# Block 3's o times proj as seven products, with proj's weight sums made by GpSimd in blocks 1 to 3

## What is computed

```python
x = L0_attn_x
xn = _layernorm(x, axis=-1)
# inside s: q, k, v = rmsnorm(xn) @ ternary(qkv_w).T; chunk by chunk
#   o = scale * (intra + cross);  S = lam_T * S + kv
#   o = rmsnorm(rmsnorm(o)) @ ternary(proj_w).T
s = _L0_attn_ref(xn, L0_attn_qkv_w, L0_attn_qkv_norm_w, L0_attn_proj_w, L0_attn_proj_norm_w, L0_attn_norm_w, L0_attn_s)
g = _silu(_L0_ffn_ref(xn, L0_ffn_weight, L0_ffn_bias))
x = x + s * g
```

## Time and profile before

| | before |
|---|---|
| median of 3 runs | 1307.04 us (1304.21 to 1307.58) |
| the profiled execution, its own time | 1304.94 us |
| span of the profiled execution, first to last instruction | 1303.7 us |
| busy: PE, DVE, ACT, POOL | 1271.8, 998.4, 741.1, 518.2 us |
| mean granted TensorE clock | 0.997 |

### The profile page before, as it was taken

One profiled execution on the slowest core, in us unless ns is written; L12 is line 12 of the kernel. 1 busy time (PEld: TensorE's weight loads), 2 busy tenths in 40 slices (PEclk: granted clock), 3 DMA queues, 4 the chain that ended last, 5 costly groups with the idle time before them and its releaser, 6 DMA issues.

```text
span 1303.7 us, 26389 instructions
## 1 busy us (share of the span) xinstructions
PE 1271.8 (98%) x10263; PEld 806.5 (62%) x10263; DVE 998.4 (77%) x1552; ACT 741.1 (57%) x1792; POOL 518.2 (40%) x435
## 2 busy tenths in 40 slices
PE   4999999999999999999999999999999999999998
PEld 2576867666665746657565665757566574656655
DVE  7888368677777878789777787878878787878745
ACT  5886256273554646566464566657456464646732
POOL 1430793835434334253432235242243324325161
PEclk9999999999999999999999999999999999999999
DMA  9622211303113031130402103040120404112020
GB/s 360 254 98 74 58 50 34 114 10 106 49 34 113 18 106 34 39 116 18 138 18 89 42 22 133 17 136 20 73 66 17 130 17 127 29 48 75 2 81 33
DMA packets 35677, 97.69 MB, mean 75 GB/s; under 512 B 10977, under 2 KB 11233, under 8 KB 35554
## 3 DMA queue, kind: packets, MB, share of 16 engines
q1 hardware_dynamic: 33024, 88.65, 19.8%
q10 hardware_dynamic: 2530, 7.37, 2.7%
HBM read 71.85 MB, written 16.81 MB: 68 GB/s over the span
## 4 chain that ended last, share of the span: by engine, by line
PE 85%; POOL 4%; DVE 4%; issue 3%; ACT 2%; DMA 1%; SPq 0%; DVEq 0%; POOLq 0%; ACTq 0%
PE ring L866 18%; PE ring L825 13%; PE ring L799 13%; PE ring L851 12%; PE ring L1030 10%; PE att_ps L904 4%; PE ring L1006 3%; PE att_ps L959 3%; PE ring L916 2%; PE att_ps L932 2%; PE att_ps L962 1%; DVE b_lo L1438 1%; PE ring L769 1%; DMA raw<-in_ffn_w 1%; POOL ffn_sum L2452 1%
## 5 line engine op out<-in xcount | busy, mean ns | idle before, releaser
L866 PE MATMUL ring<-b_hi,qkv_q 128*128 128x256 f16 x1216 | 268.2, 272 | 0.8 <-DVE b_lo L1438 0.8
L866 PE MATMUL ring<-b_lo,qkv_q 128*128 128x256 f16 x1216 | 268.2, 273 | 0.0
L2557 POOL TENSOR_TENSOR xt<-xt,gate_even 128x512 f32<-128x512 f32 x58 | 90.1, 1557 | 205.8 <-DVE gate_even L1626 158.0
L2535 POOL TENSOR_TENSOR sq<-sq 128x512 f32<-128x512 f32 (+1 forms) x58 | 58.0, 1000 | 239.8 <-DVE b_lo L1438 143.7
L866 PEld LDWEIGHTS ring<-b_hi,qkv_q 128*128 128x128 fp8e4 x1216 | 120.2, 99 | 17.9 <-DVE b_lo L1438 1.7
L866 PEld LDWEIGHTS ring<-b_lo,qkv_q 128*128 128x128 fp8e4 x1216 | 118.9, 98 | 14.9
L2161 ACT ACTIVATE sq<-att_ps,sq_scale 128x128 f32<-128x128 f32 x256 | 69.9, 381 | 54.3 <-DVE ow L1581 29.7
L2056 ACT ACTIVATE arena<-arena,lam_T 64x64 f32<-64x64 f32 x384 | 93.0, 329 | 4.3 <-issue 3.7
L2546 POOL TENSOR_TENSOR small<-small 128x1 f32<-128x1 f32 x32 | 19.6, 614 | 162.2 <-DVE small L1633 162.2
L2523 POOL TENSOR_TENSOR stack_odd<-arena,lam_q 64x1024 f32<-64x1024 f32 x32 | 82.6, 2581 | 2.9 <-POOL xt L2557 0.3
L2077 ACT ACTIVATE gate_odd<-ring,wscale 128x512 f32<-128x512 f32 x26 | 17.9, 687 | 112.0 <-PE ring L851 112.0
(11 more groups left out here) (305 smaller groups left out, 3561.8 us busy)
## 6 DMA issues: line engine op xcount, KB each, us to landing
xt<-in_x SPq DMA_DIRECT2D x60, 512.0 KB, 4.0
out<-xt SPq DMA_DIRECT2D x31, 512.0 KB, 2.6
raw<-in_qkv_w SPq DMA_DIRECT2D x24, 512.0 KB, 15.8
arena<-arena ACTq DMA_DIRECT2D x28, 256.0 KB, 2.9
y<-in_x_turned SPq DMA_DIRECT2D x14, 512.0 KB, 5.8
y_odd<-in_x_turned SPq DMA_DIRECT2D x14, 512.0 KB, 6.7
raw<-in_ffn_w SPq DMA_DIRECT2D x8, 512.0 KB, 10.0
norm_rows<-norm_out SPq DMA_DIRECT2D x14, 256.0 KB, 5.9
```

The source lines that it names most:

```text
L866: ins = pe.matmul(ring[:, b, e * BT:(e + 1) * BT], qkv_q[:, cb, o:o + P], part[:, cb, :], start=(cb == 0 and part is b_hi and (e == 0 or i ...
L2535: pool.tensor_tensor(sq[:, 0, 0:m, :], sq[:, 0, 0:m, :], sq[:, 0, m:2 * m, :], ALU.add).then_inc(s_sqw, 1)
L2557: pool.tensor_tensor(o, o, gate_of(i)[:, c, cs], ALU.add).then_inc(s_add, 1)
```

## The change

`BY_PRODUCTS` goes from 4 to 3, so block 3's o is multiplied by proj as seven products as well. The four sums of proj's weights move on GpSimd: T1 from block 3, before `decay_q(3, 0)`, to the end of block 1's list, behind `sum_squares(1, 1)`; T2 from behind `decay_q(3, 1)` to block 2, behind the norm factors; T4 from block 4 to block 2's `attention(2, 0)`, behind the sum T3 of k; T3 from block 4 to block 3's `attention(3, 0)`. Two waits in `decay_q` that stood for the old places take the ordinary form.

```diff
@@ -374,7 +374,7 @@
-        BY_PRODUCTS = 4
+        BY_PRODUCTS = 3
@@ -2511,11 +2511,11 @@
                 elif c == 1 and is_first(g - 1):
-                    pool.wait_ge(*((s_zeros, 2) if i == 0 else (s_pwsum, 3)))
+                    pool.wait_ge(s_zeros, CHUNKS)
...
                 elif c == 0:
-                    pool.wait_ge(*((s_pwsum, 1) if i == BY_PRODUCTS - 1 else (s_add, of_out(i - 1, 1, 1))))
+                    pool.wait_ge(s_add, of_out(i - 1, 1, 1))
@@ -2570,7 +2570,7 @@
                     if i == BY_PRODUCTS - 1:
-                        sum_proj_weights("T2")
+                        sum_proj_weights("T4")
                     if i == BY_PRODUCTS:
                         sum_proj_weights("T3")
@@ -2587,6 +2587,8 @@
                     sum_squares(i, 1)
+                    if i == 1:
+                        sum_proj_weights("T1")
@@ -2643,6 +2645,8 @@
                         norm_scale(i + 1, 0)
                         norm_scale(i + 1, 1)
+                    if i == 2:
+                        sum_proj_weights("T2")
@@ -2659,10 +2663,6 @@
                         add_out(i - 1, 1, 1)
-                        if i == BY_PRODUCTS - 1:
-                            sum_proj_weights("T1")
-                        if i == BY_PRODUCTS:
-                            sum_proj_weights("T4")
                         decay_q(i, 0)
                         decay_q(i, 1)
```

## The result

| | kernel before | changed kernel |
|---|---|---|
| median of 22 runs each, us | 1307.96 (1303.17 to 1309.62) | 1308.99 (1308.42 to 1311.28) |
| profiled execution, us (its span) | 1304.94 (1303.7) | 1308.73 (1307.5) |

The ratio is 1.0016, 95% interval [1.0008, 1.0023]: slower by 1 to 3 us, and within the 0.3% that was called "no change". The forecast was +1.4 us and 1308.4 us. The number was right, and that was in part luck. The sum behind it left out a wait of over 2 us in the changed kernel and one of 3 us in the kernel before, which stand against each other.

The account below looks back on a forecast made before the run. PE's matmuls were taken to bound the kernel. Terms of -0.82 (fewer matmuls), +2.2 (T1 holding DVE) and 0 (other sums) gave +1.4 us on the 1307.04 median: 1308.4 us, range 1304.8 to 1311.0.

Parts of the forecast that it names:

- What bounds the kernel: All blocks: PE's matmuls set a stretch's length, and another engine matters only where it is late for PE.
- Part 1: Blocks 3 and 4: 8 fewer PE matmuls, less what the border gives back, -0.82 us; bounds -1.73 and 0.
- Part 2: Start of block 2: T1 holds DVE 3.3 us, `diag` comes late and PE waits, +2.2 us; bounds 0 and 3.1.
- Part 3: T2 and T4 in block 2, T3 in block 3: their delays stay hidden from PE, 0 us; bounds 0 and 1.5.
- So PE doesn't see it: Block 2: T2 may hold DVE 3.83 us, but `b_sum_lo` has 11 us spare and the decayed q 6.6 us.
- T4's thin cover: Block 2: T4 delays the squares, whose sum ends at 274.3 while PE wants it at 274.79, 0.5 us spare.
- no other PE wait over 0.6 us: Profile after: besides block 2's wait of about 2.2 us ahead of L991, no PE wait exceeds 0.6 us.
- DVE has the old T2 in its way there today and is rid of it, so I take 0: Block 3: T3 may hold DVE 3.83 us, masked scores have 2.7 us spare, old T2 is gone; 0 us.
- T1 hidden: Rival, start of block 2: DVE isn't held at T1, only the matmul saving counts, 1306.2 us; chance 0.17.
- T2 ahead of `o_lo`: Rival, block 2: T2 starts first, `o_lo` and PE stand up to 3.83 us, +5.2 us, 1312.2; chance 0.07.
- Thin covers: Rival: T4 makes the squares or T3 the masked scores late by about 1 us, some 1309.7 us; chance 0.13.
- misfit: Rival, block 3: the seven products' first two find a bank or `o_lo` not ready, 1309.0 us; chance 0.05.

Follow-up runs that it names:

- e10: Changed kernel with T1, T2 behind block 2's k sums and first squares, T4, T3 behind block 3's decayed q and first squares, v's additions ahead of masked scores: 1303.55 us.
- e11: Kernel before with only T1 moved from ahead of block 3's decayed q to behind block 2's first chunk's squares: 1305.29 us, ratio 0.9969.
- e3: Changed kernel with T1 behind k's sums in block 2, T2 ahead of block 3's decayed q, T4 behind them, T3 behind block 3's first squares: 1304.77 us.
- e1: Kernel before with only T1 moved to the end of block 1's GpSimd list: 1308.31 us, ratio 0.9996.
- e6: Kernel before with T1 moved to the end of block 1's list and computed twice in a row: 1313.3 us in one run.
- e5: Kernel before plus a GpSimd write of T1's length, reading nothing, at T1's new place; sums in old places: 1308.91 us in one run, beside 1309.87.
- e9: Kernel before with v's last additions put ahead of the masked scores in DVE's list of block 2: 1308.45 us, ratio 0.9988.
- e7: Changed kernel with v's last additions put ahead of the masked scores in DVE's list of block 2: 1306.49 us, ratio 0.9983 to the kernel before.
- e4: Changed kernel with T1 at its new place, T2 ahead of block 3's decayed q, T4 behind them, T3 behind block 3's first squares: 1307.11 us, ratio 1.0018.

## Why the prediction was right, point by point

**What bounds the kernel.** Right: in the profiles every difference between blocks 2 to 4 is a PE wait or the number or pace of its matmuls.

**Part 1, -0.82 us.** Right, mechanism and size. e10 against e11 gives -0.88 and e3 against the earlier trace rows -0.87, and the 0.54 us for `o_lo` and 0.36 us for `diag` are where the pattern of blocks 7 and 8 put them. In the changed kernel itself it is -0.45 (151.96 against 152.41), because a copy of ACT in block 3 comes 0.3 us late; this small wait comes and goes without the products too (e1, e6, e11: block 3 at 78.53 and not 78.11).

**Part 2, +2.2 us.** Right in mechanism: DVE stood for 3.27 us (forecast 3.3), and a reading sum does it where a writing one doesn't (e1, e5). The size varies with the execution: 1.35, 1.38, 1.46, 1.77, 2.00 and 2.00 us in six profiles. In the changed kernel's profile the term that was too large is L1633's delay, 2.5 us forecast and 1.78 measured against the block's start: GpSimd's squares, and T1 behind them, began 0.6 us earlier in the block than in the earlier trace rows (`sq_sum` at 1.63 in place of 2.26). The term that was missing is the clock: behind the waits of 2.00 us and of 4.76 it fell to 0.50 and cost about as much again as the shorter of them; behind those of 1.35 to 1.77 it stayed at 1.00.

**Part 3, 0 us.** Wrong, and this is the step that failed. "So PE doesn't see it" was argued for T2 from the users of `b_sum_lo` and of the decayed q. I followed the k sums to their own users and not to whom they hold while they run. `centre` stands beside `k_sum_last`, `add_v` begins 6.50 us behind the end of that sum (in the four profiles above; in e3, where y lands behind the sum's start, later still), and PE's p4 had 0.77 us to spare. The rows for it stood in the earlier trace rows, as the proof that such a sum holds DVE. It cost 2.15 us; "no other PE wait over 0.6 us" was wrong by it. T4's thin cover held: the squares start at 273.54 behind ACT and not behind T4, and L982 doesn't wait. A step of `centre` in block 3 (L1348) takes 4.85 us beside T3, where the same step on the other half takes 1.65, and PE doesn't see it.

**What offset it.** "DVE has the old T2 in its way there today and is rid of it, so I take 0" was wrong too. T1 and T2 of the kernel before, in block 3, cost 3.03 us plus 0.51 for a copy of ACT behind it in the executions in which y lands late (e5, e9; the block is 3.83 us longer). The profile that I read was one in which it landed early. Against its 1304.9 us the changed kernel's profile is 3.8 us longer; against a stretch of 81.94 us for block 3, as in e5 and e9, it would be level: +3.97 - 6.63 + 2.35 = -0.3 us, worked out from those stretches. The measured difference of medians, +1.0, lies between. I had noted that the profile lay 2.1 us under the median and only carried the offset along; by the times above it was most likely the missing wait, which no profile of this kernel shows.

**The rivals.** T1 hidden: false for the sum, true for a write. T2 ahead of `o_lo`: not in the profile of the changed kernel, but seen in e7, with 2.55 us of PE time. It needed GpSimd to gain on DVE, which a fallen clock does. That the 6 slowest of the changed kernel's 22 runs (1310.77 to 1311.28) are such executions is likely and not shown. Thin covers and misfit: neither came.

## What to carry to other kernels

Where two engines exclude each other, an instruction that is moved has a second price beside its own length: it shifts the later ones, and each of these may hold other work than before, so follow every shifted instruction to whom it holds and not only to who reads its result. Put long GpSimd sums of SBUF tiles where DVE has PSUM work or none, as behind a chunk's squares here, and not around a step whose start hangs on a DMA. When the profiled execution is faster than the median by more than the change is worth, find the wait that the profile doesn't show before summing against it.

## What the hardware showed that I had not expected

- A wait of PE can cost nearly twice its length: 2.00 us idle, then 3.4 us at a granted clock of 0.50 (matmuls of 256 columns 0.213 us apart in place of 0.109), 1.7 us more. Idle times of 1.35 to 1.77 us at the same place left it at 1.00, and so did 2.15 and 3.03 us ahead of v's p4. Nor does the length decide alone: ahead of block 1's L991 PE is idle for 3.57 us in the kernel before, and the clock falls to 0.50, and for 3.58 us in e4, where it stays at 1.00. What sets these apart isn't settled.
- DVE and GpSimd hand over in turn when both have two-input work queued: 0.5 us in the landing of one DMA turned the order of the next ones round and made L1414 3.9 us later.
- A GpSimd write of 128x4096 fp8 (3.51 us) left DVE's two-input instructions at their 0.16 and 0.69 us.
